# A graph message pass with mixture-of-experts: the opening reordered, and the first message item multiplied in two passes

## What is computed

```python
x1 = layernorm(x)[src].reshape(-1, 16, 32)
x2 = edge_attr_512.reshape(-1, 16, 32)
contrib = path_coeffs[None, :, None] * x1[:, i1, :] * x2[:, i2, :]      # 64 paths (i1, i2, i3)
edge_out = zeros(20000, 16, 32).at[:, i3, :].add(contrib)
x = x + zeros(625, 512).at[dst].add(edge_out.reshape(-1, 512))
```

## Time and profile before

| | us |
|---|---|
| median of 3 runs | 1065.06 (1063.54 to 1066.51) |
| profiled execution | 1068.3 |
| its span | 1067.1 |
| DVE busy | 562.2 (53%) |
| PE busy | 886.1 (83%) |
| POOL busy | 349.0 (33%) |

### The profile page before, as it was taken

How to read it: one execution, slowest core, us unless ns; L and a number is a source line. 1 busy time by engine, 2 the same in 40 slices (tenths; PEclk the granted TensorE clock), 3 DMA queues, 4 the chain that set the end, 5 groups by cost and what they waited for, 6 DMA issues and landing times.

```text
span 1067.1 us, 20286 instructions
## 1 busy us (share of the span) xinstructions
PE 886.1 (83%) x7194; PEld 479.9 (45%) x7195; DVE 562.2 (53%) x1321; ACT 225.9 (21%) x579; POOL 349.0 (33%) x390
## 2 busy tenths in 40 slices
PE   0267677678677677799999999999997999999988
PEld 0033333334333333485464644646444445454455
DVE  5499999999999999576211111111110221211116
ACT  1032232232233231341211111111210211212100
POOL 3655434434534520012323232232232232332120
PEclk9999999998999999999999999999998999999999
DMA  8857657657657654666999999999999999999918
GB/s 255 290 201 234 213 195 233 213 197 240 201 198 245 201 195 159 264 240 236 383 393 397 395 393 399 387 394 387 391 392 405 376 398 395 394 394 396 373 61 321
DMA packets 70341, 321.04 MB, mean 301 GB/s; under 512 B 12879, under 2 KB 13032, under 8 KB 48315
## 3 DMA queue, kind: packets, MB, share of 16 engines
q1 hardware_dynamic: 48021, 260.82, 64.1%
q0 software_dynamic: 21248, 56.55, 16.3%
q10 hardware_dynamic: 934, 1.80, 0.6%
HBM read 308.55 MB, written 13.62 MB: 302 GB/s over the span
## 4 chain that ended last, share of the span: by engine, by line
PE 57%; DVE 18%; issue 11%; DVEq 9%; POOL 1%; DMA 0%; ACT 0%; another core or an unknown queue 0%; POOLq 0%; ACTq 0%
PE ps L1241 21%; DVE big L603 15%; PE ps L1287 11%; PE ps L867 7%; DVEq L601 4%; DVEq L594 4%; PE ps L1185 4%; PE ps L622 3%; PE ps L894 3%; PE ps L1234 2%; PE ps L1261 1%; PE ps L1259 1%; DVEq L603 1%; PE ps L1281 1%; POOL big L339 1%
## 5 line engine op out<-in xcount | busy, mean ns | idle before, releaser
L603 DVE TENSOR_TENSOR big<-big 128x512 f32 (+1 forms) x640 | 384.7, 673 | 17.1 <-DMA big<-xn_d,idx 14.5
L622 PE MATMUL ps<-big,mixed 128*32 128x256 f32 x2512 | 170.7, 412 | 131.4 <-DVE big L603 122.3
L1241 PE MATMUL ps<-big 128*64 128x512 f32 x1024 | 239.9, 611 | 14.1 <-issue 14.0
L339 POOL DMA_INDIRECT big<-xn_d,idx x157 | 169.2, 1078 | 201.4 <-DVE big L603 144.7
L622 PEld LDWEIGHTS ps<-big,mixed 128*32 128x32 f32 x2512 | 79.7, 116 | 227.4 <-DVE big L603 143.1
L1146 POOL DMA_INDIRECT big<-h_d,idx x64 | 62.9, 983 | 361.0 <-issue 276.7
L1251 DVE TENSOR_TENSOR mixed<-big,ps 128x256 f32<-128x256 f32 x64 | 26.9, 421 | 270.1 <-ACT big L1248 269.8
L1241 PEld LDWEIGHTS ps<-big 128*64 128x64 f32 x1024 | 69.3, 139 | 139.6 <-issue 134.1
L1287 PE MATMUL ps<-big,mixed 128*64 128x256 f32 x1024 | 124.6, 385 | 0.1
L1202 POOL DMA_INDIRECT y_d<-big,sia x74 | 75.3, 1017 | 122.9 <-DVE big L1300 69.5
L1287 PEld LDWEIGHTS ps<-big,mixed 128*64 128x64 f32 x1024 | 67.9, 136 | 35.5 <-issue 2.9
(11 more groups left out here) (212 smaller groups left out, 670.7 us busy)
## 6 DMA issues: line engine op xcount, KB each, us to landing
big<-in_L_ffn_Wg SPq DMA_DIRECT2D x64, 1024.0 KB
big<-in_L_ffn_Wu SPq DMA_DIRECT2D x64, 1024.0 KB
big<-in_L_ffn_Wd SPq DMA_DIRECT2D x64, 1024.0 KB
big<-in_edge_attr SPq DMA_DIRECT2D x39, 1024.0 KB
big<-y_d SPq DMA_DIRECT2D x10, 768.0 KB, 12.0
big<-xn_d,idx POOLq DMA_INDIRECT x157
big<-in_L_ffn_sWg SPq DMA_DIRECT2D x2, 1024.0 KB, 5.0
big<-in_L_ffn_sWu SPq DMA_DIRECT2D x2, 1024.0 KB, 7.1
```

Of the source, the lines that this page charges most:

```text
L339: pool.indirect_dma_start(xs[s][:, c, :], None, xn_d[:, :], bass.IndirectOffsetOnAxis(ap=table[:, c0 + c:c0 + c + 1], axis=0)).then_inc(x_ ...
L603: ins = dve.tensor_tensor(pr[k % 2][:, 0:chunks, EXT * p:EXT * (p + 1)], xs[s][:, 0:chunks, ds(o1, EXT)], es[s][:, 0:chunks, ds(o2, EXT)], ...
L622: ins = pe.matmul(edge_bank(k // 2)[WIN * h:WIN * (h + 1), h0:h0 + HP * EXT], onehot[s][:, CW * h + r, :], pr[k % 2][:, CW * h + r, :], st ...
L1241: ins = pe.matmul(bank(k2)[TA * h:TA * (h + 1), :].rearrange("p (w f) -> p w f", w=2), xgT[k2][:, k, 0:TA], gu[:, :, k, W * h:W * (h + 1)] ...
```

## The change

- x is loaded in two pairs of transfers, blocks 0 to 2 and blocks 3 to 4, each with a semaphore; the first edge quarter follows on SP at once. The statistics of blocks 0 to 2 wait for the first only.
- The other three edge quarters are issued on SP behind its store of xn, and the router, fill_rows and fill_pairs on ACT after ACT's part of the store has landed. ACT does one square root of a constant early.
- POOL gathers chunks 0, 4, 8 and 12 of item 0 first, with a semaphore of their own (x_first_in), then the other nine.
- Item 0 becomes two steps u = 0 and u = 1. Step 0 does all eight parts of products for the four chunks first in their quarters, into disjoint places of pr, so without waits for part_used; step 1 does the other nine. Each has its own contraction, eviction, turn and selection; the selection of both adds up in the same bank. Step 1 has a filler matmul with a zeroed one-hot chunk for the fourth quarter. From there on item t is step t + 1 in all counts.
- The gathers of item 1 wait for the end of step 0 and then run three a part of step 1. The first three no longer go ahead unreleased.

```diff
+    x_first_in = sem("x_first_in")
+    def gather_sources(s, table, c0, until=None, chunks=range(EC), landed=None):
+        for c in chunks:
+            if until is not None and c % PER == 0:
                 pool.wait_ge(part_ok, until + c // PER)
             pool.indirect_dma_start(xs[s][:, c, :], None, xn_d[:, :],
                                     bass.IndirectOffsetOnAxis(ap=table[:, c0 + c:c0 + c + 1], axis=0)
+                                    ).then_inc(x_in[s] if landed is None else landed, 16)
-    s_x, n_x = load(sync, "ld_x", *rows(lambda r: (X[r, :, :], x.rearrange("(b p) d -> p b d", p=BP)[r])))
+    x_first, x_last = load_x("ld_x_a", 0, BA_), load_x("ld_x_b", BA_, NB)
+    load_edges(0, 0, quarters=range(1))
...
+    G(pool.memset(onehot[0][:, EC0, :], 0.0))
...
-    s_wr, n_wr = load(act, "ld_router", (wr[:, :, :], w_router.rearrange("(p k) e -> p k e", k=KT)))
-    act.wait_ge(G.sem, g_const)
-    s_zero, n_zero = load(act, "fill_rows", (y_d[N * YR:, :], es[0][TC:TC + (P - BP) * YR, CW * FQ, :]))
-    s_fill, n_fill = load(act, "fill_pairs", (pair_d.rearrange("(p r) c -> p r c", r=LPP), fill[:, :, :]))
+    act.wait_ge(G.sem, 3)
+    act.activation(wmax[0:1, 0:1], ones[0:1, 0:1], ACT.Sqrt)
...
-    sync.wait_ge(s_x, n_x)
-    sync.wait_ge(G.sem, g_const)
-    load_edges(0, 0, quarters=range(2), short=True)
...
     sync.wait_ge(V.sem, ln1[NB - 1])
+    s_xb, n_xb = store_rows(sync, "st_xn_b", BA_, NB)
+    sync.wait_ge(G.sem, g_rest)
+    load_edges(0, 0, quarters=range(1, QW), short=True)
+    act.wait_ge(s_xa, n_xa)
+    s_wr, n_wr = load(act, "ld_router", (wr[:, :, :], w_router.rearrange("(p k) e -> p k e", k=KT)))
+    act.wait_ge(G.sem, g_const)
+    s_zero, n_zero = load(act, "fill_rows", (y_d[N * YR:, :], es[0][TC:TC + (P - BP) * YR, CW * FQ, :]))
+    s_fill, n_fill = load(act, "fill_pairs", (pair_d.rearrange("(p r) c -> p r c", r=LPP), fill[:, :, :]))
...
-    rows_stored(sync)
-    load_edges(0, 0, quarters=range(2, QW), short=True)
-    sync.wait_ge(x_in[0], 16 * EC0)
+    sync.wait_ge(x_in[0], 16 * (EC0 - QW))
...
-    gather_sources(0, idx, 0, chunks=EC0)
+    heads = range(0, EC0, CW)
+    gather_sources(0, idx, 0, chunks=heads, landed=x_first_in)
+    gather_sources(0, idx, 0, chunks=[c for c in range(EC0) if c not in heads])
...
+    def step(t):
+        return t + 1
+    def item(u):
+        return max(u - 1, 0)
+    def of_chunks(u, mem, chunks):
+        if at(u, 0):
+            return mem[:, 0:EC0:CW, :]
+        if at(u, 1):
+            return mem[:, 0:CW * FQ, :].rearrange("p (h r) d -> p h r d", r=CW)[:, :, 1:CW, :]
+        return mem[:, 0:chunks, :]
+    def products_of(u, k, chunks):
+        if at(u, 0):
+            return pr[k % 2][:, QW * (k // 2):QW * (k // 2) + QW, :]
+        return of_chunks(u, pr[k % 2], chunks)
...
             if k == 0:
                 dve.wait_ge(e_in[s], edges)
-                dve.wait_ge(x_in[s], sources)
-            if k > 1 or not at(t, 0):
-                dve.wait_ge(part_used, SUB * t + k - 1)
+                dve.wait_ge(x_first_in if at(u, 0) else x_in[s], sources)
+            if not at(u, 0):
+                dve.wait_ge(part_used, SUB * u + k - 1)
...
+        if at(u, 0):
             for h in range(QW):
+                ins = sums_over(h, CW * h, pr[k % 2][:, QW * (k // 2) + h, :], True, True)
+        elif at(u, 1):
+            sums_over(FQ, EC0, iotaw[:, 0:HP * EXT], True, True)
+            for r in range(1, CW):
+                for h in range(FQ):
+                    ins = sums_over(h, CW * h + r, pr[k % 2][:, CW * h + r, :], r == 1, r == CW - 1)
...
-    for t in range(NG):
+    for u in range(step(NG)):
+        t = item(u)
         s = t % 2
         if 0 < t < NG - 1:
-            load_edges(1 - s, SHORT + t * GE, SUB * t)
-        if t < NG - 1:
-            gather_sources(1 - s, idx, EC * (t + 1), SUB * t)
+            load_edges(1 - s, SHORT + t * GE, SUB * u)
+        if u > 0 and t < NG - 1:
+            gather_sources(1 - s, idx, EC * (t + 1), SUB * u)
```

More of the change, by code:

```diff
@@ L333, in gnn_moe @@
     PER = 3
-    def gather_sources(s, table, c0, until=None, chunks=EC):
-        for c in range(chunks):
-            if until is not None and c % PER == 0 and (c > 0 or not at(until, 0)):
+    x_first_in = sem("x_first_in")
+    def gather_sources(s, table, c0, until=None, chunks=range(EC), landed=None):
+        for c in chunks:
+            if until is not None and c % PER == 0:
                 pool.wait_ge(part_ok, until + c // PER)
@@ L588, in place_rows, with products @@
         act.activation(place, place, ACT.Relu, scale=-1.0, bias=ones[:, 0:1]).then_inc(place_ok, 1)
-    def products(t, s, edges, sources, chunks=EC):
+    def step(t):
[12 more added lines that the diff above has]
+        return of_chunks(u, pr[k % 2], chunks)
+    def products(u, s, edges, sources, chunks=EC):
         for k in range(SUB):
@@ L608, in products, with contract, sums_over @@
                     dve.memset(opening[:, PER * k + p // PER:PER * k + p // PER + 1], 0.0)
-    def contract(t, s, k, chunks=EC):
+    def contract(u, t, s, k, chunks=EC):
         h0 = HP * EXT * (k % 2)
-        pe.wait_ge(part_ok, SUB * t + k + 1)
-        if k == 0:
+        pe.wait_ge(part_ok, SUB * u + k + 1)
+        if k == 0 and not at(u, 1):
             pe.wait_ge(oh_ok, t + 1)
-        if k % 2 == 0 and (k > 2 or not at(t, 0)):
-            pe.wait_ge(evt_ok, PARTS * t + k // 2 - 1)
-        for r in range(CW):
-            for h in range(QW):
-                if CW * h + r >= chunks:
-                    continue
-                ins = pe.matmul(edge_bank(k // 2)[WIN * h:WIN * (h + 1), h0:h0 + HP * EXT],
-                                onehot[s][:, CW * h + r, :], pr[k % 2][:, CW * h + r, :], start=r == 0,
-                                stop=r == min(CW, chunks - CW * h) - 1)
+        if k % 2 == 0 and (k > 2 or not at(u, 0)):
+            pe.wait_ge(evt_ok, PARTS * u + k // 2 - 1)
+        def sums_over(h, c, products, first, last):
+            return pe.matmul(edge_bank(k // 2)[WIN * h:WIN * (h + 1), h0:h0 + HP * EXT], onehot[s][:, c, :], products,
+                             start=first, stop=last)
+        if at(u, 0):
+            for h in range(QW):
+                ins = sums_over(h, CW * h, pr[k % 2][:, QW * (k // 2) + h, :], True, True)
[4 more added lines that the diff above has]
+                    ins = sums_over(h, CW * h + r, pr[k % 2][:, CW * h + r, :], r == 1, r == CW - 1)
+        else:
+            for r in range(CW):
+                for h in range(QW):
+                    if CW * h + r >= chunks:
+                        continue
+                    ins = sums_over(h, CW * h + r, pr[k % 2][:, CW * h + r, :], r == 0,
+                                    r == min(CW, chunks - CW * h) - 1)
@@ L655, in select @@
             ins = pe.matmul(bank(BS)[:, P * f:P * (f + 1)], evT[:, P * f:P * (f + 1)], sel[:, qq, :],
-                            start=qq == 0 and f == 0, stop=qq == PARTS - 1 and f == FPP - 1)
+                            start=qq == 0 and f == 0 and not at(u, 1),
+                            stop=qq == PARTS - 1 and f == FPP - 1 and not at(u, 0))
         ins.then_inc(sel_ok, 1)
     def evict_sums(t):
-        act.wait_ge(sel_ok, PARTS * t + PARTS)
+        act.wait_ge(sel_ok, PARTS * step(t) + PARTS)
         if not at(t, 0):
@@ L759, in more_item @@
         pool_ready()
-        gather_sources(1, idxx, 0, chunks=chunks)
+        gather_sources(1, idxx, 0, chunks=range(chunks))
         dve.wait_ge(added_ok, NB * x + NB + 1)
@@ L770, in more_item @@
         for qq in range(PARTS):
[L771 to L776 removed]
+            contract(u, t, 1, 2 * qq, chunks)
+            contract(u, t, 1, 2 * qq + 1, chunks)
+            evict(u, qq)
+            turn(u, qq)
+            evict_turned(u, qq)
+            select(u, t, qq)
         evict_sums(t)
```

96 lines of the change are left out of this document (48 added, 48 removed).

## The result

| | median of 5 runs, us | lowest, highest |
|---|---|---|
| kernel before | 1065.06 | 1062.29, 1066.51 |
| changed kernel | 1071.23 | 1070.23, 1074.60 |

The ratio is 1.0074, 95% interval 1.0052 to 1.0096: the change makes the kernel slower, by 7.9 us (5.5 to 10.2) of the ratio or 6.2 us of the medians. The forecast was 1066.5 with a range of 1059 to 1073, and "the same" as the likeliest class; the time lies in the range, and in the class (slower by over 0.3%) that had a chance of 0.31.

What follows compares the result with a forecast made beforehand. VectorE was taken to bound the message phase. Start 30.0 plus passes of 20.9 and 24.8 plus 1.0 of wait puts item 1 at 76.7 against 75.3, 1.4 us slower: 1066.5 us, 8-in-10 range 1059 to 1073.

Steps and rivals of the forecast that it cites:

- x, statistics, the store: Opening: x lands at 8.93 as now, statistics take 1.2 instead of 3.06 us, the store lands at 20.2 instead of 22.3.
- S: Start of pass one's first product: 30.0 us, bounds 28.0 to 32.5, where the kernel before starts at 42.9.
- the sum of bytes: DMA after the store: 2.9 MB of edges and fills plus 1.0 MB of gathers take 11.0 us, until 29.5 plus landing.
- late edges or fill: Rival at the opening: edges or fill_pairs land only at 33 to 34, S is 33.5, total 1070; chance 0.12.
- Pass one: Item 0's 64 products of 128 elements: sequencer-bound at 2.6 us a part, 20.9 us, bounds 20.6 to 23.0.
- register work hides: Rival in pass one: register loads run beside the previous part's products, 14 us for the pass, total 1059.5; chance 0.13.
- Pass two: Item 0's 64 products of 288 elements: 3.1 us a part, 24.8 us, low 24.0, high 26.4.
- Item 1's sources: Sixteen gathers during pass two, 1.25 or 1.52 us apart: wait before item 1 of nothing or 1.6 us, taken as 1.0.
- What comes later is moved as a block: After the message phase: later PE and DMA work starts when that phase ends and only shifts with it.
- The forecast's own range: Change in item 1's start without the rivals: -2.4 to +4.2 us, total 1062.7 to 1069.3; forecast chance 0.60.
- the slow rivals: Two rivals slower than the forecast: gathers locked out in pass two (1072, chance 0.15), late edges or fill (1070, chance 0.12).
- the lock-out: Rival in pass two: item 1's last gathers are held until DVE stops, item 1 starts 7.1 us later, 1072; chance 0.15.

Runs made afterwards that it cites:

- e3: The changed kernel's new opening alone, with item 0 in one pass and thirteen gathers in order as in the kernel before; 1061.25 us, ratio 0.9989.
- e11: The changed kernel, unedited, run again on the third chip; 1091.05 us, ratio 1.0110 against the kernel before on that chip.
- e2: The changed kernel with the router, fill_rows and fill_pairs put back ahead of ScalarE's store; 1067.45 us, ratio 1.0040.
- e7: e2 with fixed columns in pass one, so no register loads or operations there (computes something else); 1084.33 us, one execution, second chip.
- e8: e2 without the one-element memsets (openings) in pass two that let gathers in; 1088.57 us, one execution, second chip.
- e4: The two passes of item 0 alone, with the opening as in the kernel before; 1070.63 us, ratio 1.0064.
- e1: The kernel before, unedited, profiled a second time on the first chip; 1061.97 us, one execution.
- e6: The new opening with the fills ahead of the store and item 0 in one pass (e2's and e3's edits together); 1078.04 us, ratio 0.9996, second chip.
- e5: e6's opening, one contraction pass, head-chunk products of four parts made ahead, item 1's edges loaded after part 3; 1079.83 us, ratio 1.0013, second chip.
- e12: The kernel before, unedited, run on a fourth chip; 1063.58 us, one execution.
- e10: The kernel of e6 again, on the third chip beside e9; 1077.64 us, ratio 0.9993 against the kernel before.
- e9: e5 with only the first quarter of item 1's edges waiting for part 3, on the third chip; 1076.86 us, ratio 0.9990.

## Why the prediction came out as it did

**x, statistics, the store: right.** The last load landed at 8.94 (forecast 8.93), the store was issued at 13.77 (13.75), the first gather started at 21.83 (21.1) and the fourth at 25.82 (25.2).

**S, the first product: wrong, 35.16 for 30.0,** and outside its bounds of 28 to 32.5, which the forecast itself had named as a sign of being wrong. This is the step that failed. It is the step from the sum of bytes to S, in two terms. The first is the landing of fill_pairs, 33.57 where the sum had everything landed by about 30. The bytes themselves were about right: from 18.5 to 30.0 us the DMA engines moved 3.91 MB, where the sum had 3.9 by 29.5. But a transfer has landed when its last packet has. POOL doesn't stop at four gathers, it issues one every 1.25 us, and fill_pairs' last nine packets, 0.04 MB, took until 33.5 beside gathers that held 95% of the DMA time. The 5.5 us in the earlier trace rows became 13.16 us in that company, 13.0 in e3 and 10.22 in e11. The second term is 1.6 us that the sum had at nothing: the wait for fill_pairs stands ahead of the loop, so DVE's register load (1.11 us) and the first dispatch come behind the landing. When a gather lands last, as in e2, the registers are loaded already, and the product starts 0.26 us behind it. The two are 3.6 + 1.6 = 5.2 us. The rival "late edges or fill" was this mechanism, with a landing at 33 to 34 and a chance of 0.12, but it let S be the landing. Its right form was fill_pairs: the edges of 1024 KB landed after 8.9 us, and the last quarter, of 64 KB, at about 31. e2 puts the fills first, and S is 30.28: the rest of the working of S was right. e11 has S at 32.60, so of the 5.2 us some 2.6 aren't in every execution.

**Pass one: right, 21.1 for 20.9.** Parts 2.59 us apart for 2.6; DVE busy 13.8 us for 14. e7 shows the reason to be the sequencer. The rival "register work hides" is thereby false.

**Pass two: 25.5 for 24.8.** 3.18 us a part for 3.1. The additional address operation of the operands is there (ALU_OP, 40 ns), but it isn't what makes the part: DVE has next to no gaps in it. The parts without openings take 3.06 us (sixteen products in 6.12), as in e8, and those with openings 3.18, so the 0.1 us is the openings'. The wait of 1.00 us for TensorE in front of the pass wasn't in the sum. It cost about nothing: in e4 the same gap of 1.02 us is there with no wait named.

**Item 1's sources: 0.5 for 1.0.** The sixteen gathers started 1.36 us apart (55.54 to 75.95), between the two values weighed, and the last is in part 6, where the rival had it locked out; it took 1.02 us. The Trainium skill (SBUF — State Buffer, "SBUF: two separate sides") has the loser of the shared port fully blocked for the length of the other instruction. Beside products of 0.45 us e8's gathers show at most 0.23 us over the 0.94 of an undisturbed one, less than the length of a product, and several show none at all; of the 2.36 us at the start of an item in the earlier trace rows no run here shows the cause.

**"What comes later is moved as a block": wrong by 2.3 us.** It held to within 0.2 us from item 1 to the mark (359.5 us in the changed kernel, e2 and e4 alike, 359.7 in e1), and failed a millisecond into the run, in a block of products whose instructions didn't change.

**The sum.** S +5.2, pass one +0.2, pass two +0.7, sources -0.5: 5.6 us beyond the forecast's +1.4 makes +7.0, the +6.8 of the mark; and +2.3 for the block. The forecast's own range ended at +4.2 and so missed both; its upper end, 1069.3, lies below every run of the changed kernel. The 8-in-10 range held the time because the slow rivals had been let into it, and of these the lock-out (1072) came nearest in number with a mechanism that e8 refutes: that the time lies in the range is luck in part. (The chance of 0.31 for slower is also a little off its own terms: 0.15 + 0.12 + a tenth of 0.60 is 0.33.) The 9.3 us of the profiles and the 6.2 us between the medians both lie in the interval of the ratio, 5.5 to 10.2.

**Why the idea doesn't pay**, apart from S and the block: the wait that it removes is 12.8 us (e2 against e1), and the second pass costs 77.47 - 30.28 = 47.2 us in place of 32.4, 14.8 more. The fixed costs of a part, 1.1 us for its registers and about 1.5 us for dispatching eight products, hide under eight products of 416 elements (4.06 us), and in pass two under eight of 288 (3.06 us), but not under eight of 128. By e7's 1.68 us a part, pass one would take 13.4 us by the engine alone and takes 21.1, so some 7.7 of the 14.8 us are the sequencer's. Most of the rest is the engine's own fixed time, some 0.09 us an instruction, for 64 instructions more. The gain comes with the time per element, and the loss with the time per instruction.

## What to carry to other kernels

Splitting a step of an engine to start it earlier pays its cost per instruction again; read that cost from the sequencer's rows and not from the engine's, and compare it to the wait before anything is built. A transfer that is moved out of idle time into a busy stretch has a new landing time, to be worked out with all that every queue starts until its last packet has landed, and it should be checked which instruction waits for it, and what has still to be done behind that wait. And when an execution is longer by more than the shifted stretch explains, compare untouched blocks one by one, over several profiles: here all six with the second pass lose 2 to 3 us in a block that the change doesn't touch.

## What the runs showed of the hardware

**Chips differ by 14 us for the same kernel, and in how much a change costs.** On the second and third chip the kernel before takes 1078.5 us for 1064, and on the third the changed one costs 11.9 us (9.4 to 14.3) instead of 7.9. The profiles show stops of TensorE, with no wait named, ahead of contractions. This is one in e6, in item 2:

```profile
126.11 3.48 PE L631 MATMUL ps<-big,mixed 128*32 128x256 f32 x32 [2.44 <-issue]
```

The stop is 2.44 us. The granted clock is 1.00 or 0.97 up to its end and 0.50 behind it, so the contraction takes 3.48 us instead of 1.93, and DVE waits 1.12 us. Between 45 and 435 us there are eight to ten stops of over 1.6 us in each of the seven profiles of the second and third chip (e5 to e11), three in the first profile of the kernel before, and none in e1 to e4, e12 and the first profile of the changed kernel. In e6 DVE's waits of this kind in the message phase are 13.7 us, in e10 14.0, and in e1 there are none; that is the size of the 14 us. Why TensorE stops on these chips no run shows.

**The granted clock alone doesn't explain it.** In the changed kernel's first profile TensorE is granted in full through pass two, in e11 not:

```profile
60.00:65.00 5.00, 3.91 (x47) 1.00 0.68 177
```

These are 47 products in 5 us at 1.00, against 24 at 0.50, the 1.2 GHz level, in the same window of e11. In e5, too, the clock was 0.50 in 60 to 65, and in e9 0.57. But in e8, where DVE waited 7.06 us until 69.73, it was 1.00 in 60 to 65, and TensorE did its products there one by one, 0.7 us apart:

```profile
64.40 0.38 PE L655 MATMUL ps<-big,mixed 128*32 128x256 f32 x1 [0.34 <-issue]
65.14 0.39 PE L655 MATMUL ps<-big,mixed 128*32 128x256 f32 x1 [0.36 <-issue]
```

And on the first chip the clock falls as well, to 0.66 at 85 to 90 us in e1, where DVE doesn't wait for it. A two-pass item 0, whose parts are shorter, has less room under DVE for a late contraction than a one-pass one: in item 0, e10 lost 1.85 us at most in one wait where e11 lost 7.04. That this is the reason for the higher cost on the third chip is argued, not shown.

**The same transfer, issued at the same time in the same kernel, landed after 13.16 us in one execution and after 10.22 us in another,** by its last nine packets (the first profile of the changed kernel, and e11).

**A load of sixteen registers takes DVE's sequencer 1.10 us**, and it is dead time for the engine as soon as what is queued is shorter.
